# Moving the next group's differences and exponentials, and batching the work-table loads, in a graph kernel's attention passes

## The reference

```python
h = (x @ W).reshape(N, HEADS, HEAD_DIM)            # 8 heads of 32
e = (h * a_src).sum(-1)[src] + (h * a_dst).sum(-1)[dst]
e = jnp.where(e > 0, e, 0.2 * e)
m = jax.ops.segment_max(e, dst, num_segments=N)
ex = jnp.exp(e - m[dst])
denom = jax.ops.segment_sum(ex, dst, num_segments=N)
out = segment_sum(h[src] * (ex / denom[dst]), dst) + b
```

## Time and profile before

| | us |
|---|---|
| median of 3 runs (lowest to highest) | 8629.59 (8629.22 to 8640.47) |
| the profiled execution's own time | 8623.56 |
| its span, first to last instruction | 8621.7 |
| mean granted TensorE clock | 0.817 |
| first attention pass, loop and ends, about | 5905 to 7212 |
| second attention pass, about | 7336 to 8583 |

### The profile page before, as it was taken

The page is one execution under the profiler, slowest core; times in us unless marked ns, Lnnn a source line. Parts: engine busy times, 40 slices in busy tenths (PEclk is TensorE's granted clock), DMA queues, the critical chain, the costliest instruction groups (busy, mean ns, idle before and its releaser), DMA issues. The chain is left out here.

```text
span 8621.7 us, 114948 instructions
## 1 busy us (share of the span) xinstructions
PE 6160.1 (71%) x25212; PEld 4605.7 (53%) x25213; DVE 5075.3 (59%) x9533; ACT 2537.0 (29%) x5700; POOL 4101.0 (48%) x4374
## 2 busy tenths in 40 slices
PE   3877778765366666699999999955666665577775
PEld 1446666654144444366666666633555553455554
DVE  4248888873433332266666666665666666566666
ACT  0135555542200000233333333333333332233332
POOL 0036666640077775043444444414666661666663
PEclk9988878878577787699999999976777777677777
DMA  3257777771033333143443443423444441544443
GB/s 117 112 182 230 234 234 234 232 208 37 18 105 105 105 105 80 45 125 111 119 120 113 119 120 111 120 55 117 127 135 134 125 133 45 150 137 139 138 139 94
DMA packets 440460, 1100.92 MB, mean 128 GB/s; under 512 B 102512, under 2 KB 177365, under 8 KB 439479
## 3 DMA queue, kind: packets, MB, share of 16 engines
q0 software_dynamic: 249344, 763.23, 31.6%
q1 hardware_dynamic: 190636, 333.56, 11.7%
HBM read 1014.51 MB, written 81.94 MB: 127 GB/s over the span
## 5 line engine op out<-in xcount | busy, mean ns | idle before, releaser
L765 POOL DMA_INDIRECT st_rows<-g_table,st_stage_idx x1632 | 1561.5, 957 | 861.4 <-issue 459.1
L2429 PE MATMUL st_psM<-st_msg,st_hot 128*128 128x273 f32 x3264 | 962.4, 456 | 265.3 <-DVE st_msg L2276 265.3
L859 POOL DMA_INDIRECT st_rows<-kv_table,st_stage_idx x832 | 846.7, 1018 | 482.1 <-issue 233.5
L705 POOL DMA_INDIRECT st_rows<-p_table,st_stage_idx x816 | 841.8, 1032 | 302.9 <-issue 220.3
L2429 PEld LDWEIGHTS st_psM<-st_msg,st_hot 128*128 128x128 f32 x3264 | 714.4, 224 | 469.2 <-issue 161.9
L765 POOL DMA_INDIRECT st_rows<-h_table,st_stage_idx x816 | 775.9, 951 | 244.4 <-issue 236.3
L1555 DVE TENSOR_TENSOR st_pre<-st_psP,st_rows 128x512 f32<-128x512 f32 x816 | 524.0, 683 | 536.5 <-PE st_psP L1646 393.4
L1652 PE MATMUL st_psC<-st_w,st_rT 128*128 128x256 f32 x3264 | 815.0, 393 | 0.0
L1652 PEld LDWEIGHTS st_psC<-st_w,st_rT 128*128 128x128 f32 x3264 | 587.5, 190 | 373.8 <-ACT st_rT L1613 212.3
L1462 PE MATMUL st_psM<-st_rows,st_hot 128*128 128x256 f32 x1632 | 500.1, 475 | 385.1 <-DMA st_rows<-h_table,st_stage_idx 188.3
L1608 ACT ACTIVATE st_gate<-st_pre 128x256 f32<-128x256 f32 x816 | 340.4, 417 | 1288.0 <-DVE st_pre L1555 1287.8
(11 more groups left out here) (399 smaller groups left out, 11737.0 us busy)
## 6 DMA issues: line engine op xcount, KB each, us to landing
st_dst_row<-in_dst_row SPq DMA_DIRECT2D x310, 512.0 KB, 5.6
kv_table<-st_rows_out SPq DMA_DIRECT2D x25, 1560.0 KB, 5.6
st_ea<-in_ea SPq DMA_DIRECT2D x103, 256.0 KB, 3.8
st_rows<-g_table,st_stage_idx POOLq DMA_INDIRECT x1632
st_pens<-pen_table SPq DMA_DIRECT2D x208, 72.0 KB
st_rows<-kv_table,st_stage_idx POOLq DMA_INDIRECT x832, 5.0
st_rows<-h_table,st_stage_idx POOLq DMA_INDIRECT x816
st_rows<-p_table,st_stage_idx POOLq DMA_INDIRECT x816, 3.7
```

Of the source, the lines that this page charges most:

```text
L705: pool.indirect_dma_start(out=rows[:, u * SLOTS + j, :], out_offset=None, in_=table, in_offset=bass.IndirectOffsetOnAxis(ap=stage_idx[:, u ...
L765: pool.indirect_dma_start(out=rows[:, slot, j, :], out_offset=None, in_=table, in_offset=bass.IndirectOffsetOnAxis(ap=stage_idx[:, g, u * ...
L859: pool.indirect_dma_start(out=rows[:, slot, j, :], out_offset=None, in_=kv_table, in_offset=bass.IndirectOffsetOnAxis(ap=stage_idx[:, g, u ...
L2429: last = nc.tensor.matmul(out[:, 0:MSG_W], onehots[:, j, :], msg[:, n, j, :], start=(j == 0), stop=(j == SLOTS - 1))
```

## The change

1. DVE: `differences` of group q + 1 are made between `combine(s + 1)` and `combine(s + 2)` of group q. `diff` gets two buffers.
2. ACT: the exponentials of group q + 1 (`weights`) stand behind the factors of s + 1, and row one-hot 2 of group q + 2 stands behind them, ahead of the factors of s + 2.
3. DVE reads block and number of extras of all three supertiles in one load behind the first messages. The numbers of the extras are loaded by every engine only inside the branch for extras.
4. PE: `expanded` is raised behind the extras by one more matmul of 2 columns with zeros; so `edge_scores` drops its load and its wait for `x_expanded`.
5. `columns` is gone; all one-hots read `iota_row` in SBUF.

```diff
+    def extras_of(eng, row):
+        _, values = nc.values_load_multi_w_load_instructions(
+            work[0:1, ds(row, 1), 0:2].squeeze(1), engines=[eng.engine], min_val=-1, max_val=NS * NB,
...
+    def blocks_of(eng, row, count=1):
+        _, values = nc.values_load_multi_w_load_instructions(
+            work[0:1, ds(row, count), 2:4], engines=[eng.engine], min_val=0, max_val=NS * NB,
...
-            diff = st.sb("diff", [P, SLOTS, U, H3])
+            diff = st.sb("diff", [P, 2, SLOTS, U, H3])
+            zeros = st.sb("zeros", [P, 2], F32R)
-            columns = psU[:, 512 - P:512]
...
-                        _, x1, _, _ = work_of(dve, U * q + U)
                         dve.wait_ge(S["expanded"], START + U * q + U)
-                        dve.wait_ge(S["x_expanded"], START + x1)
...
-                        one_hot(hot[:, u, :, :], dst_of(s), columns).then_inc(S["onehot"], 1)
+                        one_hot(hot[:, u, :, :], dst_of(s)).then_inc(S["onehot"], 1)
...
-                    def combine(s, n, ahead, ahead_u):
-                        x0, x1, b0, more = work_of(dve, s + 1)
+                    def combine(s, n, ahead, ahead_u, block):
+                        b0, more = block
...
                         with dve.If(more):
+                            x0, x1 = extras_of(dve, s + 1)
...
+                    def differences(i, g):
+                        q = 2 * i + g
+                        dve.wait_ge(S["back_ps"], START + q + 1)
+                        hold(dve, held)
+                        v.tensor_tensor(diff[:, g, :, :, :], et[:, :, :, :], group_view(psW), ALU.subtract).then_inc(S["diffed"], 1)
...
                         messages(i, g, 0)
+                        blocks = blocks_of(dve, s + 1, U)
...
+                        combine(s + 1, (g + 1) % 2, s + U + 1, 1, blocks[1])
+                        if ahead:
+                            differences(i + g, 1 - g)
+                        combine(s + 2, g % 2, s + U + 2, 2, blocks[2])
...
-                        act.wait_ge(S["diffed"], START + q + 1)
-                        nc.scalar.activation(group_view(psU), diff[:, :, :, :], ACT.Exp).then_inc(S["weights"], 1)
                         message_columns(i, g, 0)
...
                         if ahead:
                             make_hotrow(q + 2, 1)
+                        make_factors(s + 1)
+                        if not last:
+                            weights(i + g, 1 - g)
+                        if ahead:
                             make_hotrow(q + 2, 2)
-                        make_factors(s + 1)
                         make_factors(s + 2)
...
-                        bring(hotrow[:, u, :, :], block_number(b0), u == 0).then_inc(S["expanded"], 1)
+                        bring(hotrow[:, u, :, :], block_number(b0), u == 0)
                         with pe.If(more):
+                            x0, x1 = extras_of(pe, s + 1)
...
+                        at = u * 2 * H3
+                        nc.tensor.matmul(psE[:, at:at + 2], hotrow[:, u, 0, :], zeros[:, :], start=False, stop=True,
+                                         skip_group_check=True).then_inc(S["expanded"], 1)
```

More of the change, by code:

```diff
@@ L738, in work_of @@
         return at_least_zero(eng, values, NS * NB)
+    def extras_of(eng, row):
+        _, values = nc.values_load_multi_w_load_instructions(
+            work[0:1, ds(row, 1), 0:2].squeeze(1), engines=[eng.engine], min_val=-1, max_val=NS * NB,
+            skip_runtime_bounds_check_because=BOUNDED)
+        return at_least_zero(eng, values, NS * NB)
+    def blocks_of(eng, row, count=1):
+        _, values = nc.values_load_multi_w_load_instructions(
+            work[0:1, ds(row, count), 2:4], engines=[eng.engine], min_val=0, max_val=NS * NB,
+            skip_runtime_bounds_check_because=BOUNDED)
+        return [(values[2 * n], values[2 * n + 1]) for n in range(count)]
     def block_number(b):
@@ L2315, in _ @@
                     segment_maxima(0, 0)
+                    differences(0, 0)
                     with dve.Fori(0, TURNS - 1) as i:
                         for g in range(2):
-                            group(i, g, True)
-                    group(TURNS - 1, 0, True)
-                    group(TURNS - 1, 1, False)
+                            blocks = first_half(i, g, True)
+                            second_half(i, g, True, blocks)
+                    blocks = first_half(TURNS - 1, 0, True)
+                    second_half(TURNS - 1, 0, True, blocks)
+                    blocks = first_half(TURNS - 1, 1, False)
+                    second_half(TURNS - 1, 1, False, blocks)
                 @block.scalar
@@ L2341, in make_extra_hotrows @@
                         for u in range(U):
-                            x0, x1, b0, more = work_of(act, U * q + u + 1)
+                            (b0, more), = blocks_of(act, U * q + u + 1)
                             with act.If(more):
+                                x0, x1 = extras_of(act, U * q + u + 1)
                                 with act.Fori(x0, x1) as x:
@@ L2373, in message_columns, with weights, group @@
                             msg[:, slot % 2, :, 0:GAT_W].rearrange("p j (h c) -> p j h c", h=H3)[:, :, :, HW3 - 1],
-                            diff[:, :, u, :], ACT.Exp).then_inc(S["msg_cols"], 1)
-                    def group(i, g, ahead):
+                            diff[:, g, :, u, :], ACT.Exp).then_inc(S["msg_cols"], 1)
+                    def weights(i, g):
+                        act.wait_ge(S["diffed"], START + 2 * i + g + 1)
+                        hold(act, held)
+                        nc.scalar.activation(group_view(psU), diff[:, g, :, :, :], ACT.Exp).then_inc(S["weights"], 1)
+                    def group(i, g, ahead, last=False):
                         q = 2 * i + g
                         s = 6 * i + U * g
-                        act.wait_ge(S["diffed"], START + q + 1)
-                        nc.scalar.activation(group_view(psU), diff[:, :, :, :], ACT.Exp).then_inc(S["weights"], 1)
                         message_columns(i, g, 0)
@@ L2398, in _ @@
                         make_extra_hotrows(q)
+                    weights(0, 0)
                     with act.Fori(0, TURNS - 1) as i:
@@ L2402, in _ @@
                     for g in range(2):
-                        group(TURNS - 1, g, False)
+                        group(TURNS - 1, g, False, g == 1)
                 @block.tensor
@@ L2408, in expand @@
                         s = U * q + u
-                        x0, x1, b0, more = work_of(pe, s + 1)
+                        (b0, more), = blocks_of(pe, s + 1)
                         def bring(onehots, b, fresh):
@@ L2439, in scatter_extra @@
                     def scatter_extra(s, n):
-                        x0, x1, _, more = work_of(pe, s + 1)
+                        (_, more), = blocks_of(pe, s + 1)
                         with pe.If(more):
+                            x0, x1 = extras_of(pe, s + 1)
                             with pe.Fori(x0, x1) as x:
```

31 lines of the change are left out of this document (16 added, 15 removed).

## The result

The changed kernel takes 8697.01 us (median of 4 runs, 8684.53 to 8701.96) against 8629.4 for the kernel before: a ratio of 1.0075, interval 1.0057 to 1.0092. It is 68 us slower. The profiled execution took 8697.2 us, span 8695.3, TensorE clock 0.814. The loss lies in the attention passes: from the first to the last messages they last 1280.6 and 1231.0 us, before 1253.0 and 1196.3.

The account below looks back on a forecast made before the run. No engine is at a limit, so waits set the time. Terms -35 + 11 + 11 + 80 + 4 + 57 - 31 - 20 = +77 us on 8629.6 give 8706, taken as 8705; range 8640 to 8785.

Parts of the forecast that it names:

- back_ps: Extra DVE wait for PE's transposes when s + 1 has an extra: 16 groups by 0.67 us, 11 us lost.
- Part 1, the head: Head of a group on DVE: exponential waits and differences go, 92 us at most; 57 taken back for PE, 35 us gained.
- The further 20 us for gathers that start earlier: Where exponentials were late, earlier messages start waiting gathers earlier: about 8 chains of 2.6 us, 20 us gained.
- Part 2, loads: DVE's load before the third rescaling goes, differences replace it: counted as nothing; branch loads and transposes cost 11 us each.
- the 11 us for the branch's load and the zero matmuls: ACT's load before an extra's row one-hot and three 2-column matmuls: about 0.8 us in 14 groups, 11 us lost.
- Part 3, ACT's queue: Row one-hot 2 ahead of the factors of s + 2 makes DVE wait 1.6 us, 50 times: 80 us lost.
- The deduction of 31 us: In the 26 groups waiting for rows, DVE's new delays, some 1.2 us net, disappear in the wait: -31 us.
- Part 4, the ports: One-hots reading SBUF hold POOL's gathers, 0.6 us mean each: 57 us where scores wait for rows, plus 4 for one-hots.
- More idle time before L2206 for rows: Sign that the forecast is right: DVE's scores wait longer for gathered rows; no size given.
- The loop's top: DVE's pauses at the attention loops' top, 181.3 us, 131.7 in pass one, set by the code's place: left unchanged.

Follow-up runs that it names:

- a: Kernel before with only the one-hots' operand changed: they read `iota_row` in SBUF instead of its PSUM copy; 8658.36 us, ratio 1.0030.
- e: Run a plus only the head's move: differences between second and third rescaling, exponentials behind the factors of s + 1, row one-hots still ahead of these; 8658.94 us.
- b: Changed kernel with row one-hot 2 back ahead of the factors of s + 1 on ACT; 8627.04 us, ratio 0.9995 to the kernel before.
- g: Run b with ACT reading the whole work row in one load ahead of an extra's row one-hot, instead of two loads; 8637.83 us.
- f: Run b without the zero matmuls: the expansion's own matmul raises `expanded`, DVE loads the number of extras and waits for them itself; 8636.02 us.
- c: Changed kernel with the PSUM copy of `iota_row` back and a DVE wait for the exponentials ahead of the third rescaling; 8676.26 us.
- i: Kernel before with three small DVE memsets ahead of the first pass's loop, nothing else; 8575.18 us, ratio 0.9935.
- d: Run b with the PSUM copy of `iota_row` back and the DVE wait for the exponentials, as in c; 8635.97 us.
- j: Changed kernel with three small DVE memsets ahead of the first pass's loop; 8650.16 us, ratio 1.0024 to the kernel before.
- h: Run b with f's and g's edits, and first and second rescaling's one-hots reading columns in PSUM, the third's SBUF; 8540.01 us, ratio 0.9901.
- l: Run b with h's one-hot columns and two small memsets placing the loop; zero matmuls and ACT's two loads stay; 8547.12 us.
- k: Run h with 125 small DVE memsets ahead of the first pass's loop; 8608.02 us, ratio 0.9970 to the kernel before.

## Why the prediction was right, and where it wasn't

The forecast was 8705, the measurement 8697, with the direction right. The chain of runs shows that its terms were not all right, and that the errors cancelled: that the number is within 8 us is luck, that the change is slower and where it loses is not.

| step | forecast | measured | by |
|---|---|---|---|
| one-hots in SBUF | 57 + 4 | +26 | a |
| head, with `back_ps` | -35 + 24 + 11, less 20 | +5 | e against a |
| loads, zero matmuls | -24 + 11 | -35 | b against e |
| ACT's queue | 80, less 31 | +69 | change against b |
| sum | +77 | +65 | |

The 24 us are the differences' own time. The forecast took them out of the head and set them in their new place against the load that goes ("I count this as nothing"); in e they have moved and the load is still there (30.1 us of "issue" before L2217), so there they count in full.

- **Part 1, the head.** "Left: 35 us" failed. The 68 us of waits did go. I had taken back 57 for a longer wait for PE, and PE took 17; but rows took 35 and the transposes 28. The scores wait for rows, whose gathers hang on messages of the group before, and DVE came to them earlier only to wait longer. The further 20 us for gathers that start earlier don't show either.
- **Part 2, loads.** The "issue" before the third rescaling went as forecast (32.4 to 6.5 us). Two things went otherwise. The pauses at the loop's top became 14 us shorter, which no term had. And the 11 us for the branch's load and the zero matmuls aren't a loss: taking either out (g, f) shortens the wait for PE by 51 and 23 us and gains nothing. The price of a load was wrong as well: 0.49 us on ACT in the new form, not 0.31. The wait for the transposes is right in kind and number (18 times for 16), but 1.7 us each and not 0.67.
- **Part 3, ACT's queue.** Right in mechanism and place, too small in size: 99.0 us of waiting where 80 were forecast, 48 waits of 1.9 us on average where 50 of 1.6 were worked out, and 16 of 0.5 where an extra on s + 2 was to hide them. The factors came at 4.3 us and not 3.9, mainly because the stretch from the exponentials' start to the one-hot's, put at 0.75 us, took 1.05 (6111.51 to 6112.56). The deduction of 31 us, delays that disappear in the wait for rows, fits in size: of the 99, 70 reach the end.
- **Part 4, the ports.** The mechanism is right: the held gather ends 0.81 us behind the one-hot, with 1.79 us. The Trainium skill's rule (page "SBUF — State Buffer", section "SBUF: two separate sides") is borne out by run a, where only an operand's place differs and the gathers' busy time rises by 99 us, and by run c, where it falls back. It is borne out in one direction only, for no one-hot is held by a gather that started first. Mis-sized were both factors of the 57 us: 99 us of stretch where 151 were reckoned, since 135 gathers are held long and not 252, and 26 us that reach the end where the share of groups that wait for rows would give 38. "More idle time before L2206 for rows" holds for run a (+52), not for the whole change (-19), where DVE comes to the scores later.
- **The loop's top.** Left unchanged in the forecast; the pauses of the first pass are 20 us shorter in the change (131.3 to 110.8), and why isn't shown. Right that the place of the code makes the difference between the passes in the main; i shows 56 us that were to be had for nothing.

## What to carry to other kernels

Where two chains share an engine, ask which answers stand behind the job that you move: a 2.3 us job put ahead of a 0.6 us answer cost 70 us here, as much as the whole wait that the change had removed. Don't book a removed wait as a gain until you have named what ends last behind it; here it was the gathered rows, which took 35 of the head's 67 us. Before comparing two versions of a kernel with a long loop, look at the pause at the loop's top: three instructions more or less ahead of it were worth 0.65%, nearly as much as the change itself (0.75%).

## What the runs showed of the hardware that wasn't expected

The pause at the top of DVE's loop depends on where the loop starts. The position of its first instruction (counted in the compiled program, 64 bytes each) and the "issue" time of the first pass:

| kernel | position | us of pauses |
|---|---|---|
| before, a, g | 1469 | 131.7, 131.7, 133.5 |
| changed, b | 1469 | 115.6, 118.2 |
| e | 1470 | 132.2 |
| c, d | 1470 | 117.1, 117.5 |
| f | 1471 | 121.8 |
| i, j, h, l | 1472 | 62.5, 65.4, 66.7, 66.4 |
| k | 1597 | 136.6 |

The positions fit a code that comes in transfers of 8192 bytes, 128 instructions, of which one begins at 1472 and one at 1600: the slow starts 1469 to 1471 and 1597 lie one to three instructions ahead. Where the transfers begin is worked out, not seen, and the runs speak for the distance of 128 alone: neither 1472 nor 1600 is a multiple of 128, though k's expectation calls 1600 one. Transfers of that size in the DMA records, marked there as instructions (start behind the end of DVE's last instruction, length, in us; those of the other engines are among them) at one loop's top each:

```
before  pause 8.35: +0.7 (0.5)  +1.3 (0.9)  +6.5 (0.3)
i       pause 4.63: +0.8 (0.3)  +1.5 (1.8)
```

With the bad start a last transfer comes 5 us later, and DVE goes on 1.5 us behind it. It is so at all 15 turns: each pause of the kernel before has one such transfer more than the same turn's in i (42 against 27 in all). The Trainium skill, page "Runtime: NRT & Kernel Launch", section "Instruction fetch mechanics", has the fetch behind a taken branch; these runs add that a loop's start just ahead of the beginning of a transfer costs one transfer more at every turn. Among the slow starts there are two levels: 131.7 to 136.6 us where ACT makes one load ahead of an extra's row one-hot (before, a, e, g, k), 115.6 to 121.8 where it makes two (changed, b, c, d, f). g and b differ in nothing else. Why ACT's code should matter to DVE's pauses stays open.

Another surprise is the price of small loads. On ACT a load of two numbers of a work row takes 0.49 us and the load of all four 0.31, in the same kernel too (run g has both, 0.49 and 0.31); on DVE it is 0.54 for two, 0.34 for four and 1.45 for six. Batching saves a load only where this is hidden, as DVE's is behind 2.28 us of messages. Why fewer numbers take longer isn't shown.
